# Context products moved from the slot stage to the mamba stage through DRAM, the context root put into the exponential's scale, and a tile loop with one more step of lag

## Time and profile before

| | |
|---|---|
| runs | 1690.17, 1690.95, 1692.47 us, median 1690.95 |
| the profiled execution | 1693.12 us, its span of instructions 1690.9 us |
| busy over the span | PE 87%, DVE 74%, POOL 71%, ACT 65% |
| mean granted clock of PE | 0.941 of 2.4 GHz |
| mamba stage, to 907 us | DVE and POOL busy 96% and 95% in its middle |
| slot stage, 907 to 1493 us | first scores read by DVE at 940 us; PE busy 97% in the beats |
| expert stage | PE busy 96% from 1511 to 1669 us, last scatter at 1681 us |

### The profile page before, as it was taken

One profiled execution on the slowest core, in us unless ns is written; L12 is line 12 of the kernel. 1 busy time (PEld: TensorE's weight loads), 2 busy tenths in 40 slices (PEclk: granted clock), 3 DMA queues, 4 the chain that ended last, 5 costly groups with the idle time before them and its releaser, 6 DMA issues. The chain is left out here.

```text
span 1690.9 us, 21625 instructions
## 1 busy us (share of the span) xinstructions
PE 1473.7 (87%) x6178; PEld 878.9 (52%) x6178; DVE 1259.1 (74%) x2137; ACT 1096.9 (65%) x2149; POOL 1194.6 (71%) x852
## 2 busy tenths in 40 slices
PE   3888889888998889988885899999999999839994
PEld 1333334333343334333332577777777777639883
DVE  2899999999999999999992366666666666634542
ACT  3777887778877787777863566566666665414442
POOL 1899999999999999999993115455455545435665
PEclk8899999999999999999997899999999999959997
DMA  4355445454545545544441622022022000036671
GB/s 154 130 174 164 157 151 182 157 165 154 170 162 165 167 151 170 169 156 157 152 129 35 253 83 110 14 116 112 17 111 109 21 1 14 12 108 178 189 199 50
DMA packets 105846, 214.17 MB, mean 127 GB/s; under 512 B 12162, under 2 KB 56709, under 8 KB 105744
## 3 DMA queue, kind: packets, MB, share of 16 engines
q1 hardware_dynamic: 101200, 204.50, 37.3%
q0 software_dynamic: 4544, 8.47, 1.5%
HBM read 168.28 MB, written 45.56 MB: 126 GB/s over the span
## 5 line engine op out<-in xcount | busy, mean ns | idle before, releaser
L317 POOL TENSOR_TENSOR hc<-state,c_rows 128x1024 f32<-128x1024 f32 x256 | 598.2, 2360 | 43.1 <-DVE state L485 39.3
L485 DVE TENSOR_TENSOR_SCAN state<-ps_da,inp 128x512 f32<-128x512 f32 x512 | 593.5, 1206 | 27.2 <-ACT ps_da L397 27.2
L574 PE MATMUL ps_y<-hc,ident 128*128 128x512 f32 x1024 | 498.4, 632 | 71.8 <-POOL hc L317 71.8
L397 ACT ACTIVATE ps_da<-dt,a_neg 128x512 f32<-128x512 f32 x512 | 344.4, 687 | 124.6 <-DVE state L485 119.3
L574 PEld LDWEIGHTS ps_y<-hc,ident 128*128 128x128 f32 x1024 | 203.1, 203 | 344.1 <-issue 224.6
L474 DVE TENSOR_TENSOR inp<-dtx,ps_b 128x1024 f32<-128x1024 f32 x192 | 230.5, 1201 | 35.4 <-POOL dtx L292 23.2
L885 POOL TENSOR_TENSOR rs<-ms,m_half 128x4 f32<-128x4 f32 x48 | 49.4, 1029 | 251.2 <-DVE ms L1117 251.2
L304 POOL TENSOR_TENSOR inp<-dtx,b_rows 128x1024 f32<-128x1024 f32 x64 | 151.0, 2359 | 0.1
L527 PE MATMUL ps_misc<-x1T,w_conv 128*128 128x512 f32 (+3 forms) x256 | 120.0, 614 | 31.1 <-ACT x1T L343 22.6
L403 ACT COPY ps_b<-b_rows 128x512 f32<-128x512 f32 x192 | 111.3, 579 | 48.7 <-DVE inp L474 46.9
L1028 ACT ACTIVATE ex<-sc,nmx 77x128 f32<-77x128 f32 x192 | 74.7, 390 | 90.8 <-DVE nmx L1126 90.8
(11 more groups left out here) (211 smaller groups left out, 2646.6 us busy)
## 6 DMA issues: line engine op xcount, KB each, us to landing
b_rows<-bc_rows SPq DMA_DIRECT2D x128, 512.0 KB, 4.8
c_rows<-bc_rows SPq DMA_DIRECT2D x128, 512.0 KB, 4.0
sorted_x<-pad_rows SPq DMA_DIRECT2D x8, 4160.0 KB, 12.8
w<-in_L_ffn_W SPq DMA_DIRECT2D x78, 256.0 KB, 3.5
xrow<-sorted_x SPq DMA_DIRECT2D x39, 130.0 KB, 2.2
x_tok<-in_x SPq DMA_DIRECT2D x16, 256.0 KB, 3.9
ctx<-in_ctx SPq DMA_DIRECT2D x16, 154.0 KB
out_x<-orow,target POOLq DMA_INDIRECT x78, 2.9
```

Of the source, the lines that this page charges most:

```text
L317: pool.tensor_tensor(hc[:, n % RING], state[:, n % RING], over_c(c_rows[:, slot, n % 2]), ALU.mult).then_inc(hc_ready, 1)
L397: act.activation(ps_da[u % DA_RING][:], dt[:, par, c], ACT.Exp, scale=a_neg[:, c, n:n + 1]).then_inc(da_ready, 1)
L485: dve.tensor_tensor_scan(state[:, n % RING, c], ps_da[u % DA_RING][:], inp[:, n % RING, c], 0.0, ALU.mult, ALU.add).then_inc(state_ready, 1)
L574: ins = pe.matmul(ps_y[:, c], ident[:], hc[:, n % RING, c], start=False, stop=n == NS - 1)
```

## The change

**Mamba stage.** The context products are made here, for the group that is being scanned, in five units: P transposes the raw context of four batches (77 columns each) into ctxT; K is one matmul of 308 columns with kq_w; V0, V1 and V2 are matmuls with 128, 128 and 52 rows of the 308 as weights and vw_w as 384 moving columns. They use the same two banks. PE makes them at n = 5, 9, 13, 14 and 15, ACT reads them at n = 6, 10, 14, 15 and 0 of the next group, and SP stores the results to DRAM (kq_rows, vw_rows) and loads the context, between its loads of B and C. z0 moves from n = 9 to n = 11. xT changes its bank from 0 to 1, and the waits that guard the banks move with it: xT waits for abs1, z0 and x1 of earlier groups, xb0 for V2's read, dt0 for P's. The slot stage's weights are loaded and folded before the first group: seven more DMAs on SP before x's second, six transposes and two matmuls on PE after dt1, and five instructions on ACT ahead of the first decay. The convolution of the first group waits for four of DVE's 11 preparations instead of all. Three of the weight tiles lie in hc, with two waits of POOL for it.

**Slot stage.** The fold, the units P, K and v, and the normed context are gone; tp0 and tp1 stay. kq and vw come from DRAM (a kq, a vw and a context load per lane and pair; SP waits for the last z of the pair that used the buffer). `norm_ctx` becomes `root_ctx`, without the product, in beats 2 and 4. As the root r is positive, the scores stay unscaled, and r enters as the exponential's scale, in the negated maximum (L1126) and in a new product rser = rse * r that `weights` reads. `sum_ctx` writes to eight places and waits less. SP's Fori over the pairs is unrolled.

**Expert stage.** POOL roots j-4 first and then stores j-6; ACT norms j-5.

```diff
+    UNITS = ["P", "K", "V0", "V1", "V2"]
+    UNIT_ROWS = [min(P, GB * M - k * P) for k in range(3)]
+    PE_UNIT = {5: "P", 9: "K", 13: "V0", 14: "V1", 15: "V2"}
+    ACT_UNIT = {6: "P", 10: "K", 14: "V0", 15: "V1"}
+    BANK = {"P": 0, "K": 1, "V0": 0, "V1": 0, "V2": 0, "xT": 1, "z0": 1, "xb0": 0, "xb1": 1, "z1": 0, "dbl": 1, "dt0": 0, "dt1": 1, "out": 0, "var": 1}
...
+            sp.dma_start(kq_rows[g], kq_out[:]).then_inc(kq_stored, 16)
...
+            sp.dma_start(vw_rows[g, 0:2 * P].rearrange("(k p) f -> p k f", p=P), vw_out[:, 0:2]).then_inc(vw_stored, 16)
...
+                if pair == SLOTS and not first:
+                    store_vw_rest(g - 1)
             if not last:
                 store_rows(g + 1, 1 - par)
+                load_ctx(g + 1)
...
+                if pair == 1:
+                    store_kq(g)
+            store_vw(g)
...
+        def read_unit(g, name):
+            act.wait_ge(u_full, unit(name, g))
+            bank = ps_misc[BANK[name]]
+            if name == "P":
+                act.copy(ctxT[:], bank[:, 0:GB * M]).then_inc(u_read, 1)
+            elif name == "K":
+                need(act, kq_stored, 16 * g)
+                act.activation(kq_out[:], bank[:, 0:GB * M], ACT.Copy, scale=w_slot[:, 0:1]).then_inc(u_read, 1)
+            else:
+                k = int(name[1])
+                need(act, vw_stored, 32 * g)
+                act.copy(vw_out[0:UNIT_ROWS[k], k], bank[0:UNIT_ROWS[k], 0:3 * P]).then_inc(u_read, 1)
...
+                if n == 0 and not first:
+                    read_unit(g - 1, "V2")
...
                     root(g - 1)
+                if n in ACT_UNIT:
+                    read_unit(g, ACT_UNIT[n])
...
+                for b in range(GB):
+                    ins = pe.transpose(bank[:, b * M:(b + 1) * M], ctx[:, b], ident[0:M, 0:M])
...
+                ins = pe.matmul(bank[:, 0:GB * M], kq_w[:], ctxT[:], start=True, stop=True)
...
+                if k == 0:
+                    pe.wait_ge(z_gated, after(C, 1, g))
+                else:
+                    pe.wait_ge(u_read, unit(f"V{k - 1}", g))
+                ins = pe.matmul(bank[0:UNIT_ROWS[k], 0:3 * P], ctxT[:, k * P:k * P + UNIT_ROWS[k]], vw_w[:], start=True, stop=True)
...
-                if n == 9:
+                if n == 11:
                     fill_z(g, 0, last)
-                if n == 11:
                     fill_z(g, 1, last)
                 if not first and n == 13:
                     variance(g - 1)
+                if n in PE_UNIT:
+                    fill_unit(g, PE_UNIT[n], last)
...
+        sp.wait_ge(kq_stored, 16 * NG)
+        sp.wait_ge(vw_stored, 32 * NG)
...
+        load_kq(0, 0)
+        load_ctx(0, 0)
         for dst, src in [
-            (wq[:], t["L0_xattn_Wq"]), (wk[:], t["L0_xattn_Wk"]), (wv[:], t["L0_xattn_Wv"]),
...
+        load_kq(0, 1)
+        load_ctx(0, 1)
+        load_vw(0, 0)
+        load_vw(0, 1)
...
+                load_ctx(q, k)
+                sp.wait_ge(pe2[k], ev(PE2, "z", (q - 1) * ITERS - 1))
+                load_kq(q, k)
+                load_vw(q, k)
...
             act.wait_ge(dve1[lane], ev(V, "nmx", it))
             for b in range(GB):
                 act.activation(ex[lane][0:M, b * P:(b + 1) * P], sc[lane][:, b * P:(b + 1) * P], ACT.Exp,
-                               bias=nmx[lane][:, b:b + 1], accum_out=se[lane][:, b:b + 1]).then_inc(exped[lane], 1)
+                               bias=nmx[lane][:, b:b + 1], scale=ctx_r[:, q % 2, lane, b:b + 1], accum_out=se[lane][:, b:b + 1]).then_inc(exped[lane], 1)
...
-            dve.tensor_scalar_mul(nmx[lane][:], mx[lane][:], -1.0).then_inc(dve1[lane], 1)
...
+            if it % ITERS == 0:
+                hold(dve, ctx_root[lane], 2 * q + 2, passed2[0])
+            dve.scalar_tensor_tensor(nmx[lane][:], mx[lane][:], -1.0, ctx_r[:, q % 2, lane], ALU.mult, ALU.mult).then_inc(dve1[lane], 1)
...
             dve.reciprocal(rse[lane][0:M], se[lane][:]).then_inc(dve1[lane], 1)
+            dve.wait_ge(dve1[lane], ev(V, "rse", it))
+            dve.tensor_tensor(rser[lane][:], rse[lane][0:M], ctx_r[:, q % 2, lane], ALU.mult).then_inc(dve1[lane], 1)
...
+            if j == 0:
+                pe.wait_ge(kq_loaded[par][lane], 16 * (q // 2) + 16)
...
+            if it % ITERS == 0 and name == "r":
+                pe.wait_ge(vw_loaded[par][lane], 16 * (it // ITERS // 2) + 16)
...
-            ended = isinstance(j, int) and j >= NJ
-            if ended and buf % 2 == 0 and within(j, 4):
+            if buf % 2 == 0 and within(j, 4):
                 root(j - 4, earlier(buf, turn, 4)[0], half - 2)
-            if within(j, 5):
-                store(j - 5, earlier(buf, turn, 5)[0])
-            if not ended and buf % 2 == 0 and within(j, 4):
-                root(j - 4, earlier(buf, turn, 4)[0], half - 2)
-        over_tiles(pool, tile, 5)
+            if within(j, 6):
+                store(j - 6, earlier(buf, turn, 6)[0])
+        over_tiles(pool, tile, 6)
...
-            if within(j, 4):
-                last, last_turn = earlier(buf, turn, 4)
-                normalised(j - 4, last, last_turn, half - 2)
-        over_tiles(act, tile, 4)
+            if within(j, 5):
+                last, last_turn = earlier(buf, turn, 5)
+                normalised(j - 5, last, last_turn, half - 2)
+        over_tiles(act, tile, 5)
```

More of the change, by code:

```diff
@@ L408, in _ @@
         copy_b(0, 0)
+        act.wait_ge(s_loaded, 16 * 7)
+        act.mul(w_slot[:], w_slot[:], SCALE).then_inc(s_copied, 1)
+        act.wait_ge(s_made, 1)
+        act.copy(wihT, ps_y[:, 0, 0:3 * P]).then_inc(s_copied, 1)
+        act.wait_ge(s_made, 2)
+        act.copy(whhT[:], ps_y[:, 1, 0:3 * P]).then_inc(s_copied, 1)
+        act.wait_ge(s_made, 3)
+        act.activation(kq_w[:], ps_da[2][:, 0:P], ACT.Copy, scale=w_input[:, 0:1]).then_inc(s_copied, 1)
+        act.wait_ge(s_made, 4)
+        act.activation(vw_w[:], ps_da[1][:, 0:3 * P], ACT.Copy, scale=w_input[:, 0:1]).then_inc(s_copied, 1)
+        act.wait_ge(s_copied, 5)
         decay(0, 0, 0, 0)
@@ L655, in slot_stage @@
     rdn = [sb(f"rdn{k}", [P, GB]) for k in range(2)]
+    rser = [sb(f"rser{k}", [M, GB]) for k in range(2)]
     at = [sb(f"at{k}", [M, T]) for k in range(2)]
@@ L1070, in body @@
                     route_tanh(beat - 3, i - 1)
-                attention_exp(a, it)
+                attention_exp(a, it, q)
                 if working:
                     gru_rest(b, it2)
-                for name in u_names(beat, 0, first, last):
-                    read_u(i, par, name)
                 gru_h(a, it)
@@ L1079, in body @@
                     attention_sq(*after_this)
[L1080 to L1086 removed]
+                if beat in (0, 1) and not first:
+                    read_u(i, beat)
+                if beat < 4 and not last:
+                    sum_ctx(i + 1, beat // 2, range(beat % 2 * 2, beat % 2 * 2 + 2))
                 if after_this is not None:
@@ L1096, in _ @@
         gru_rest(1, it)
-        read_u(NQ, 1, "tp0")
-        read_u(NQ, 1, "tp1")
+        for lane in range(2):
+            read_u(NQ, lane)
         for lane in range(2):
@@ L1314, in make_u @@
+        def make_u(i, lane):
+            need(pe, u_read, u_value(i, lane) - 1)
+            if lane == 1 and i == NQ:
+                pe.wait_ge(last_summed, 1)
+            else:
+                pe.wait_ge(post_p[lane], ev(POSTP, "res2", i - 1))
+            for b in range(GB):
+                at_col = (b % 2) * (P + NE)
+                ins = pe.matmul(ps_u[b // 2][:, at_col:at_col + P + NE], res2[lane][:, b * P:(b + 1) * P], w_rows[:], start=True, stop=True)
             ins.then_inc(u_full, 1)
@@ L1388, in body @@
                 other = b if working else None
-                if beat == 1 and not first:
-                    pe.wait_ge(u_read, u_value(i - 1, "v13"))
                 if working:
@@ L1400, in body @@
                     gate_x(b, it2, par2, "z")
-                for name in u_names(beat, 0, first, last):
-                    make_u(i, par, name, first, last)
                 gate_h(a, it, par, "hn", other, it2)
@@ L1409, in body @@
                 den_spread(a, it)
-                for name in u_names(beat, 1, first, last):
-                    make_u(i, par, name, first, last)
+                if beat in (0, 1) and not first:
+                    if i == 1 and beat == 0:
+                        pe.wait_ge(prep_v, 5)
+                    make_u(i, beat)
                 after_this = following(beat, i, par, last)
```

373 lines of the change are left out of this document (173 added, 200 removed).

## The result

The changed kernel takes 1708.31 us (median of 4 runs, 1706.96 to 1712.19) against 1691.71 us for the kernel before in the same comparison (1690.17 to 1693.12): a ratio of 1.0102, 95% interval 1.0085 to 1.0118. It is slower by 1%. The forecast was 1675 us, faster by 1%. The profiled execution of the changed kernel has a span of 1710.0 us, 19.1 longer than before's 1690.9, and 3.9 us of it are the distance of that execution from the median.

The account below looks back on a forecast made before the run. It took DVE and POOL to bound the mamba stage, a chain the beats, POOL's ring the later tiles. +6 − 28 − 2.7 + 17.5 − 8 − 1 = −16.2 took 1690.95 to 1675 us; 8-in-10 range 1658 to 1692.

Parts of the forecast that it names:

- the line on the beats: Slot stage's beats: lost context products give −2.7 us, the exponential's second pointer operand costs +17.5.
- rival E: Slot beats: PE's clock falls, a tenth at 1.2 GHz adds 47 us, a fifth on the chain; about 1685; chance 0.07.
- What bounds the beats: Slot stage: a chain from scores through exponentials to new slots and norm sets the beat, though PE is busy 507 of 524 us.
- The pointer's price: Slot stage's exponentials: 390 to 485 ns each, four on the chain, 0.38 us a beat in 48 beats, taken as +17.5.
- Mamba stage: Context units mostly fit idle time of PE and ACT: +0.4 us a group, 16 groups, +6, bounds 0 and +25.
- rival B: Mamba groups lag, one late item each, 1.7 to 2.5 us a group: 1696 to 1709, taken at 1699; chance 0.12.
- The start: Before the first group: the convolution waits for four preparations instead of eleven, −1 us; the fold is hidden, 0.
- Transition: Mamba to slot stage: fewer loads and no fold before the first scores, −26 us; the first beat −2 more.
- Tile loop: Expert stage: POOL's reordered roots and stores let tiles come every 3.73 us; net −8 us, bounds −9.5 and −3.
- rival D: Expert stage: the tile loop's gain fails, POOL's wait moves or gelu and transposes bound tiles at 4 us; 1683; chance 0.10.
- Rival A: Slot stage: the exponential's scale pointer costs nothing on the chain; 1657.5 us; chance 0.10.
- C: Slot stage: PE does bound the beats, so half of its saved work comes through; about 1650 us; chance 0.03.

Follow-up runs that it names:

- a_fill: The changed kernel plus matmuls that nothing reads, at the places and sizes of the slot stage's lost context products; 1680.64 us.
- b_nounits: The kernel before, its slot stage without context products from the third pair on, the waits kept; 1694.77 us.
- b_ptr: The kernel before, its four exponentials reading their scale through a pointer to a column of ones, same output; 1711.37 us.
- a_fillnoscale: The changed kernel with the unread filling matmuls, in the last pair too, and without the context root in exponential and negated maximum; 1662.65 us.
- b_tiles: The kernel before with only the expert stage's tile loop taken from the changed kernel; 1683.90 us.
- a_fill45: The changed kernel with unread filling matmuls in the fifth and sixth beat of a pair alone; 1701.97 us.
- a_nov12: The changed kernel with the mamba stage's products V1 and V2 made for the first group alone, the waits kept; 1704.45 us.

## Why the prediction was wrong, step by step

- **The step that failed** is the sum itself, in the line on the beats: its terms were the products' 0.45 us in three beats and the exponential's pointer, both priced at full clock. The clock stood only in rival E, at 0.07 and 10 us. It cost 555.0 − (532.6 − 9.9) = 32 us in the profiled execution (a_fill as the same beats at full clock), 27.7 on the medians. E's working had two factors. The slowed work was about right: 47 us of extra PE time were supposed, and 90 us at half the clock are 45. The share on the chain was not: a fifth was supposed, and 32 / 45 = 0.7 came through, since at 1.2 GHz PE itself is the bound of the beat, as the gapless rows after 1286.26 show. The reason given against E was that beats without products were at 1.00. Those were from the last pair of a kernel with the shorter exponentials; b_nounits shows that even there the clock falls now and then, and the changed kernel adds idle time to just those beats (in the fourth 11.26 − 9.71 = 1.5 us, instead of 1.2 in before's last pair) by its own pointer. The evidence was three beats of another kernel than the one forecast. Why the clock falls in one pair and not in the next, with the same idle time, stays open.
- **What bounds the beats** was read well: a latency chain. That is what a_fill shows most plainly, where PE does 66.82 − 60.17 = 6.7 us more in a pair and the pair is no longer.
- **The pointer's price**: 482 ns measured for 485, and on the chain 16.3 us in b_ptr and 15.0 in the changed kernel (a_fill against a_fillnoscale) for 17.5. It was put on the chain almost whole; 0.32 to 0.35 us a beat of 0.37 came. The Trainium skill's figure ("ScalarE: Activation LUTs", What ACT_TABLE_LOAD costs, 93 ns for each pointer operand) agrees with 482 − 390 = 92 ns here.
- **Beats at full clock**: a_fill's 46 beats after the first take 13.9 us more than before's; 14.8 was forecast. That it came so near is partly luck: the pointer's part was some 2.5 us too large, and the gain of 2.7 for the lost products was read from rows that didn't show it. With filling matmuls in their place and without the pointer (a_fillnoscale) the 46 beats are 508.82 − 508.07 = 0.8 us shorter than before's.
- **Mamba stage** +9.1 for +5: within its bounds, and by the place named in rival B, V1 and V2 behind the wait at 1.2 GHz. The other place named there, the read of P ahead of B's copy, costs 0.5 us at most in all. B's price of 1.7 us a group was not reached: 6.3 / 14 = 0.45 a group (0.4 was forecast), and 3.5 us at the end of the stage, where V1 waits for the read of V0, and V1 and V2 stand ahead of the last projection; the sum had left that out. The start gave 0.7 of its 1 us.
- **Transition** −25.5 for −26; the first beat gave 5.6 instead of 2, as it lost all of its extra length in this pair of traces. Against the 13.0 us of b_tiles it would have given 3.1, so a part of the 5.6 is the luck of two executions.
- **Tile loop** −7.5 for −8, and 7.1 alone in b_tiles; rival D is out.
- **Rival A** (a free pointer) is out; **C** (PE bounds the beats) is out at full clock, as b_nounits and a_fill show, and true only where the clock is low.
- **The range** ended at 1692. E had no upper bound of its own; with its chain share at one instead of a fifth it would have reached 1675 + 47 = 1722, and the range would have had to hold the measured time.

The Trainium skill ("TensorE: Matmul & The Clock Gate", Part 1: The HAM clock gate) says that the clock is set by how busy the engine has been. By it the removal of PE work speaks against this change; a_fill agrees, with 27.7 us. The page's table gives the lower level to an idle engine, and here the clock fell though PE was never idle for more than 1.33 us in one piece in the beats.

## What to carry to other kernels

An engine that isn't the bound may still hold up its own clock: before taking work off TensorE in a stage that goes by latency, look at its idle time per round after the change, and price the stage at 1.2 GHz as one of the cases. The sum of the idle time is a warning and not a measure, as a_fill45 shows. If the work must go, matmuls that nothing reads can stand in its place as long as they lie beside the chain, and they are cheap to try. And a per-row factor belongs where it is applied least often: once into the operand, not into each of 192 exponentials; where it is put in the order of its engine then decides whether it is free.

## What the runs showed of the hardware

- The clock fell in rounds whose third to fifth beats have PE busy for 9.7 to 10.2 of 11.2 to 12.4 us each, and never idle for more than 1.33 us in one piece: 0.92 over the beats of the changed kernel, 1.00 with the filling matmuls (a_fill). Filling two beats of six moved the falls to the other four.
- The mean clock of one program differs between runs, and with it the time: in a_nov12 from 0.931 at 1693.7 us to 0.920 at 1715.7. With the clock held up, the runs of a_fill lie within 2.6 us.
- At 1.2 GHz the same instructions take 1.8 times as long (scores 1.97 and 1.08, mean square 1.71 and 0.95).
- A second per-partition operand costs an activation 92 ns even where its value is 1 (b_ptr, 482 against 390 ns).
